# Moving the scaling of the gates from VectorE to ScalarE, transposing the first pair's gates later, and giving the second chunk of the expert sum its own PSUM bank

## What is computed

```python
xw = einsum('ntd,dh->nth', x, Wx) + b
h_t = tanh(xw_t + h_{t-1} @ Wh)            # 32 steps, one after the other
```

```python
xn = h * rsqrt(mean(h*h) + 1e-5) * norm_scale
vals, idx = top_k(xn @ wg + bg, 4);  gates = softmax(vals)      # spread over 16 experts: gate_full
a, b = even and odd columns of xn @ w1[e] + b1[e]
s = min(a, 7) * sigmoid(1.702 * min(a, 7)) * (clip(b, -7, 7) + 1)
t = sum_e gate_full[:, e] * (s @ w2[e] + b2[e])
out = x + (h + t)
```

## Time and profile before

| | before |
|---|---|
| median of 3 runs | 109.75 us |
| profiled execution, its own time | 109.45 us |
| its span in the trace | 107.7 us |
| PE busy | 98.9 us (92%) |
| DVE busy | 71.1 us (66%) |
| ACT busy | 62.3 us (58%) |
| POOL busy | 64.6 us (60%) |

### The profile page before, as it was taken

One profiled execution on the slowest core, in us unless ns is written; L12 is line 12 of the kernel. 1 busy time (PEld: TensorE's weight loads), 2 busy tenths in 40 slices (PEclk: granted clock), 3 DMA queues, 4 the chain that ended last, 5 costly groups with the idle time before them and its releaser, 6 DMA issues.

```text
span 107.7 us, 1714 instructions
## 1 busy us (share of the span) xinstructions
PE 98.9 (92%) x553; PEld 83.8 (78%) x553; DVE 71.1 (66%) x183; ACT 62.3 (58%) x143; POOL 64.6 (60%) x77
## 2 busy tenths in 40 slices
PE   7789999499999799999995979999999999999990
PEld 2579889498999599999994858888877777777560
DVE  0302377978769984899869998666656675576420
ACT  3255887779696584668555546645656545665000
POOL 6005439994647977199657999496665545665000
PEclk9999999999999999999999999999999999999999
DMA  2998910049900009930299106990010000000003
GB/s 75 226 364 312 396 75 0 0 93 306 384 15 0 0 21 321 317 135 0 70 295 367 59 6 135 332 353 8 0 58 0 0 0 0 0 0 0 0 4 93
DMA packets 5000, 12.97 MB, mean 120 GB/s; under 512 B 752, under 2 KB 1792, under 8 KB 4992
## 3 DMA queue, kind: packets, MB, share of 16 engines
q1 hardware_dynamic: 4672, 12.69, 35.7%
q10 hardware_dynamic: 320, 0.18, 0.6%
HBM read 12.28 MB, written 0.59 MB: 120 GB/s over the span
## 4 chain that ended last, share of the span: by engine, by line
PE 72%; DVE 15%; issue 4%; DMA 2%; ACT 2%; POOL 1%; DVEq 0%; POOLq 0%; ACTq 0%
PE psA L817 18%; PE psB L817 17%; PE psY L847 9%; PE psR L847 6%; PE psR L859 4%; PE psY L762 3%; DVE lin L705 3%; DVE act L722 3%; DVE gates_w L629 2%; DMA wx_x_sb<-in_wx_x 2%; PE psM L847 2%; PE psX L762 2%; PE psY L754 2%; PE psM L771 1%; PE psM L778 1%
## 5 line engine op out<-in xcount | busy, mean ns | idle before, releaser
L419 POOL TENSOR_TENSOR actg<-act,gate_cols 128x512 f32<-128x512 f32 x31 | 39.4, 1282 | 13.8 <-DVE act L722 11.0
L499 ACT ACTIVATE psA<-psA,lim_b1a 128x256 f32<-128x256 f32 (+1 forms) x48 | 24.0, 516 | 23.7 <-PE psA L817 23.6
L705 DVE TENSOR_SCALAR lin<-psB,one_b1b 128x256 f32<-128x256 f32 (+1 forms) x48 | 25.9, 567 | 16.5 <-PE psB L817 16.5
L722 DVE SCALAR_TENSOR_TENSOR act<-lin,psA 128x512 f32<-128x512 f32 x32 | 21.9, 685 | 1.1 <-DVE lin L705 0.2
L511 ACT ACTIVATE psA<-psA,limit_col 128x512 f32<-128x512 f32 x32 | 21.1, 659 | 0.8
L817 PE MATMUL psA<-xn_hi,w_hi 128*128 128x256 f32 (+1 forms) x48 | 19.1, 397 | 0.8 <-DVE act L722 0.6
L847 PE MATMUL psY<-actg,w_sb 128*128 128x256 f32 x64 | 16.9, 386 | 0.0
L817 PE MATMUL psB<-xn_hi,w_hi 128*128 128x256 f32 (+1 forms) x48 | 16.1, 335 | 0.0
L817 PE MATMUL psA<-xn_hi,w_lo 128*128 128x256 f32 (+1 forms) x48 | 15.5, 323 | 0.0
L817 PE MATMUL psB<-xn_lo,w_hi 128*128 128x256 f32 (+1 forms) x48 | 15.4, 321 | 0.0
L817 PE MATMUL psB<-xn_hi,w_lo 128*128 128x256 f32 (+1 forms) x48 | 15.4, 320 | 0.0
(11 more groups left out here) (95 smaller groups left out, 136.4 us busy)
## 6 DMA issues: line engine op xcount, KB each, us to landing
gate_cols<-gate_rows SPq DMA_DIRECT2D x16, 512.0 KB, 5.4
w_sb<-in_w SPq DMA_DIRECT2D x4, 512.0 KB, 7.5
w_sb<-in_w SPq DMA_DIRECT2D x4, 256.0 KB, 8.6
wx_x_sb<-in_wx_x SPq DMA_DIRECT2D x1, 320.0 KB, 5.6
wx_x_sb<-in_wx_x SPq DMA_DIRECT2D x2, 128.0 KB, 2.6
out<-yT SPq DMA_DIRECT2D x2, 128.0 KB, 4.3
out<-yT SPq DMA_DIRECT2D x1, 192.0 KB, 1.9
small_h<-in_small ACTq DMA_DIRECT2D x1, 105.0 KB, 2.7
```

Source lines behind the costliest of these rows:

```text
L419: nc.gpsimd.tensor_tensor(by_pair(actg[:, u % SUM_DEPTH, w]), by_pair(act[:, u % ACT_DEPTH, w]), gate_block(u, w), ALU.mult).then_inc(actg ...
L499: last = nc.scalar.activation(psA[u % 2][:, o], psA[u % 2][:, o], ACT.Relu, scale=-1.0, bias=lim_b1a[:, e0 + k:e0 + k + 1])
L705: last = nc.vector.tensor_scalar(lin[:, v % 2, o], psB[v % 2][:, o], one_b1b[:, e0 + k:e0 + k + 1], LIMIT + 1.0, ALU.add, ALU.min)
L722: nc.vector.scalar_tensor_tensor(act[:, v % ACT_DEPTH, 0:w], lin[:, v % 2, 0:w], 1.0 - LIMIT, psA[v % 2][:, 0:w], ALU.max, ALU.mult).then_ ...
```

## The change

Four things change. `gates_scale` leaves VectorE; ScalarE gets `scale_gates`, a scaled copy with the same input and output, which waits for a new semaphore `inv_ready` that the reciprocal gives. It stands at the end of slots 0, 6, 10 and 14, after the slot's second tanh. TensorE's transposes of pair 0 move from between `up(1, 0)` and `up(1, 1)` to behind `up(1, 1)`. ScalarE's copies of pair 0 move from before slot 1's gelu to after its last tanh. Chunk 0 sums in psY, chunk 1 in psR, and the last chunk in psY and psM; chunk 1 waits for the end of the recurrence instead of `add_h(0)`, and the last chunk also waits for `add_h(0)`.

```diff
+        inv_ready = sem("inv_ready")
...
+        def y_bank(c):
+            return psY if c == 0 else psR
...
         def y_end(k):
             o = [slice(0, 3 * P), slice(3 * P, W)][k]
-            return o, (psM if k else psR)[:, 0:o.stop - o.start]
+            return o, (psM if k else psY)[:, 0:o.stop - o.start]
...
+            def scale_gates(q):
+                acte.wait_ge(inv_ready, q + 1)
+                for j in pair_tiles(q):
+                    last = nc.scalar.activation(
+                        gates_w[:, j, :].rearrange("p (a b e) -> p a b e", a=3, b=2)[:, :, 0, :],
+                        gate_sum[:, j, :].rearrange("p (a e) -> p a e", a=1).to_broadcast([P, 3, E]),
+                        ACT.Copy, scale=inv[:, j:j + 1])
+                last.then_inc(scale_done, 1)
...
-                if u < LAG:
-                    for q in at(GATES_T, u):
-                        copy_gates(q)
                 acte.wait_ge(relu_done, u + 1)
...
                 for t in steps_at(u, 1):
                     tanh(t)
-                if u >= LAG:
-                    for q in at(GATES_T, u):
-                        copy_gates(q)
+                for q in at(GATES, u):
+                    scale_gates(q)
+                for q in at(GATES_T, u):
+                    copy_gates(q)
...
             def gates_inverse(q):
                 settled()
-                mark(nc.vector.reciprocal(inv[:, 2 * q:2 * q + 2], den[:, 2 * q:2 * q + 2]))
+                nc.vector.reciprocal(inv[:, 2 * q:2 * q + 2], den[:, 2 * q:2 * q + 2]).then_inc(inv_ready, 1)
-            def gates_scale(q): ...
...
             def close_gates(q):
                 gates_sum(q)
                 gates_inverse(q)
-                gates_scale(q)
...
-                nc.vector.tensor_tensor(yT[:, cols(c)], xT[:, cols(c)], psY[:, 0:CHUNKS[c] * P],
+                nc.vector.tensor_tensor(yT[:, cols(c)], xT[:, cols(c)], y_bank(c)[:, 0:CHUNKS[c] * P],
...
                     if c == 0:
                         pe.wait_ge(b2_ready, 1)
-                    elif c < NC - 1:
-                        pe.wait_ge(yT_ready, c)
+                    elif c == 1:
+                        pe.wait_ge(step_done, T)
                     else:
+                        pe.wait_ge(yT_ready, 1)
                         pe.wait_ge(m_read, psM_turn(("rstd", pair_group(NQ - 1))))
...
                 if v < LAG:
                     for t in steps_at(v, 0):
                         step(t)
-                    for q in at(GATES_T, v):
-                        transpose_gates(q)
...
                 up(v, 1, psB[v % 2], b_mm)
                 if v >= LAG:
                     for t in steps_at(v, 0):
                         step(t)
+                if v < LAG:
+                    for q in at(GATES_T, v):
+                        transpose_gates(q)
```

More of the change, by code:

```diff
@@ L823, in y_parts @@
                 if c < NC - 1:
-                    return [(slice(0, CHUNKS[c] * P), psY[:, 0:CHUNKS[c] * P])]
+                    return [(slice(0, CHUNKS[c] * P), y_bank(c)[:, 0:CHUNKS[c] * P])]
                 return [y_end(k) for k in range(2)]
```

## The result

The changed kernel has a median of **107.22 us** over four runs (106.77 to 107.29), against 109.66 us for the kernel before (109.52 to 109.85, now four runs with e1's). The ratio is 0.9768 with a 95% interval of 0.9736 to 0.9799, so it is faster. I forecast 106.95 us, 2.80 us less than before; it is 2.44 us less. The profiled execution took 107.28 us, with a span of 105.5 us where it was 107.7.

A forecast was written before the change was run, and what follows sets the result against it. TensorE is busy from 63.0 to 103.4 us, so only its stops before 63 us can be won. 1.20 - 0.05 - 0.05 + 1.70 = 2.80 us off 109.75 gives 106.95 us, range 106.4 to 108.3.

The forecast's parts named there:

- The scaling on DVE was stretched by POOL: Gate scaling on VectorE: 706 ns in the mean, held up by GpSimd on a shared port; gone on ScalarE.
- the price on ACT: Scaled copies on ScalarE: 0.23 us start to start, 0.29 for the last, 0.52 a pair; bounds 0.20 and 0.71.
- rival B: Scaling on ScalarE dearer than 0.23 us, output in strided pieces; at 0.40 an instruction, 108.3 us; chance 13%.
- Rival C: ScalarE's queue: scaling costs the full 0.71 us there, so the kernel is slower, 110.8 us; chance 4%.
- Pair 0: Slots 0 to 2: lin starts 1.40 us sooner, TensorE no longer idles, ScalarE binds next, slot 2's relu at 21.33.
- Gain 1.20 us: Slots 0 to 2: what scaling on ScalarE wins, 0.20 of TensorE's 1.40 us given back to ScalarE.
- the granted clock is 1.00 in both stretches, so no price below contains a clock: Premise from the profile's stretches (63.0 to 103.4 us, and 1.10 us from 18.80): prices need no clock correction.
- Rival A: Behind pair 0's columns: later loads delay rstd past 0.25 us slack; all 1.20 lost gives 108.15 us; chance 12%.
- Pairs 1 and 2: Slots 6, 7 and 10, 11: ScalarE's wait for the reciprocal delays relu and tanh, loss 0.05 us each.
- Pair 3: Slots 14, 15: own bank plus scaling on ScalarE start up(16, 0) at 61.34 instead of 63.04, gain 1.70 us.
- Both edits are needed together: Slots 14, 15: with the bank alone TensorE would wait until 62.30 as today and win nothing.
- Sum: Whole kernel: 1.20 - 0.05 - 0.05 + 1.70 = 2.80 us gained, 106.95 us against the median of 109.75.

The follow-up runs named there:

- e1: The kernel before, run again without any edit: 109.58 us, span 107.8.
- e2: The changed kernel, run again without any edit: 107.45 us, ratio 0.9806 to the kernel before.
- e6: The changed kernel with transposes and copies of pair 0 back in their old places: 107.31 us, ratio 0.9764 to the kernel before.
- e5: The changed kernel with the scaling back on VectorE, moves and new banks kept: 109.63 us, ratio 0.9990 to the kernel before.
- e8: The changed kernel with every scaling done twice, first copies into a spare tensor: 108.72 us, ratio 0.9922 to the kernel before.
- e10: e5 again without edit, on one chip with e9: two of four runs at 111.4 us, two at 109.9.
- e11: e7 plus VectorE's addition of chunk 0's sum two slots later: 105.94 us, ratio 0.9635 to the kernel before.
- e7: The changed kernel with ScalarE's scaling of pairs 1 to 3 behind the next slot's relus and first tanh: 106.29 us, ratio 0.9680 to the kernel before.
- e9: e3 again without edit: five of twelve runs at 111.15 to 111.67 us, seven at 109.45 to 110.07.
- e4: The changed kernel with the old banks and their waits: 107.56 us, ratio 0.9821 to the kernel before.
- e3: The kernel before with the bank edit alone, VectorE still scaling: 111.33 us, ratio 1.0157 to the kernel before.

## Why the prediction was right, point by point

**The scaling on DVE was stretched by POOL: supported, and the price on ACT right.** The eight scaled copies take 317 to 336 ns, 323 in the median, and a pair 0.55 to 0.56 us, where I took 0.52. The Trainium skill's page ScalarE: Activation LUTs, section "What ACT_TABLE_LOAD costs", had given the estimate of 319 ns, and the trace agrees. The output in strided pieces (rival B) costs nothing. Rival C is out: ACT showed no stretch beside POOL. That the stretch on DVE is the shared port was argued from the ends of instructions, with the Trainium skill's page SBUF — State Buffer, section "SBUF: two separate sides", beside it; no run took POOL away to show it.

**Pair 0: the mechanism right, the size off.** The step that failed is "Gain 1.20 us" with its premise "the granted clock is 1.00 in both stretches, so no price below contains a clock". For those two stretches, behind the rise at 17.2 us of that one profile, the premise was true. What the working took for granted is that slots 0 to 2 would find the quick products in every run. Ahead of the rise the clock column says 1.00 too, while 256-column products lie 0.21 us apart, the spacing of 1.2 GHz (213 ns), and one run later the same products at the same place lie 0.12 apart. With an early rise the stretch to `up(3, 0)` gained 1.41 us (e2), more than the 1.20, and slot 2's relu came 0.17 sooner than forecast, mostly because the tanh ahead of ACT's copies took 0.17 us to the next start (20.82 to 20.99) where the working had 0.30. With a late rise the stretch gained 0.61. e6 and e5 settle who earned it: the scaling on ACT, not the moves.

**Rival A held in single runs.** I gave it 0.25 us of slack and 12%. It did not bind in the two profiles of the changed kernel. It did in e8, e10 and e11, where PE waited 0.6 to 0.7 us for rstd, because 2.84 to 2.94 us passed from the issue of the small write to that of the loads instead of 1.46. e8 also put 0.46 us on the way to that write, which alone exceeds the slack. The changed kernel's runs spread over 1.2 us (106.65 to 107.86). The rise of PE's speed and the landing of the columns are the two sources that the profiles show; how much each adds in the eight runs without a profile is not shown.

**Pairs 1 and 2: right.** -0.02 and 0.04 us measured against 0.05 and 0.05. The wait behind the reciprocal on ACT, 1.67 us, is the one described, and e7 shows its price: the 0.48 us of PE's wait, and 0.76 us in all.

**Pair 3: right.** 1.77 us against 1.70. "Both edits are needed together" is shown from both sides: banks alone win nothing (e9's runs near 109.7, e5), scaling alone wins 0.63 us less than both (e4). PE's wait of 0.56 us at the transposes was longer than the 0.25 of the working (61.06 less 60.81), and the transposes shorter before the next product, 0.17 us instead of 0.28.

**Sum.** 0.61 + 0.02 - 0.04 + 1.77 us, less 0.16 of a later start of the head and the end of the span, is the 2.20 us between the spans. The gain by medians, 2.44 us, is 0.36 short of the forecast 2.80. The head's late rise is the part of it that the traces show: pair 0 alone lacks 0.59 in that profile. That the median still came within 0.27 us of 106.95 owes something to luck, since the working held nothing for the moment of the rise.

## What to carry to other kernels

When an edit takes a stall away, ask what the stall was covering: here a rise of TensorE's speed that falls late by chance, which cost nothing before and 0.8 us between two profiles of the changed kernel. A wait placed on an in-order engine is paid by what stands behind it, so put it behind the work that is ready (e7), and when a dependency is cut, move its former producer out of the way too (e11). Half of a joint edit can be worse than none: the bank edit alone gathered two short stops into one of 1.8 us, and lost 1.7 us in 9 of its 16 runs.

## What the runs showed that I had not expected

- Of 30 runs of kernels with a stop of 1.81 us on TensorE, and 0.26 us more behind the transposes, 12 took about 1.7 us longer. In both of these that were profiled, products then ran at the 1.2 GHz level, with a granted clock of 0.64 over 4.4 us in e3 and 0.71 over 4.3 us in e9. In e9 they first ran 0.23 us apart for about a microsecond behind the stop. Stops of 1.13 and 0.42 us, 3.6 us apart, were not followed by it in the two profiles of the kernel before, and none of that kernel's runs took more than 110.36 us.
- In the head, products ran at the spacing of 1.2 GHz up to a moment between 17.2 us (kernel before) and 20.7 us (e6) after the start of the span, another one in nearly every profile, while the column of the granted clock said 1.00. The trace holds no record of the clock ahead of that moment.
- The write of 16 KB of gates took 1.45 to 1.84 us up to the issue of the next load in 11 of 14 profiles, and 2.84 to 2.94 us in three.
